# A transformer block on one core: tile 0's modulation and turn done by TensorE, the last turn put inside a down product, one buffer moved

## The reference

```python
mod = (silu(c) @ wmod).reshape(4, 6, 1, 512)          # sa, ca, ga, sb, cb, gb
ga, gb = [(2 * (g >= 0) - 1) * maximum(abs(g), 0.25) for g in (ga, gb)]
h = layernorm(x) * (1 + ca) + sa
q, k, v = heads(h @ w_qkv.T)                           # 16 heads of 32; q, k through relu
vk = sum over tokens of [v; 1] outer k                 # linear attention
out = (vk @ q)[:-1] / ((vk @ q)[-1:] + 1e-15)
x = x + ga * (out @ w_proj.T + b_proj)
h = layernorm(x) * (1 + cb) + sb
w = top-2 of 8 experts by sigmoid(h @ gate_w.T) + router_bias, weights from the sigmoids
x = x + gb * (sum of w_e * silu(h @ W1_e) * (h @ W3_e) @ W2_e + shared expert(h))
```

## Time and profile before

| | |
|---|---|
| median of 3 runs | 1218.91 us (1217.52 to 1221.94) |
| the profiled execution, its own time | 1217.89 us |
| its span from first to last instruction | 1216.1 us |
| mean granted TensorE clock | 0.996 |
| busy: PE, PEld, DVE, ACT, POOL | 98%, 64%, 66%, 34%, 42% |
| first key product / first key and value sums | 25.41 us / 34.97 us |
| experts' stage | about 780 us to the end |

### The profile page before, as it was taken

The page is one execution under the profiler, slowest core; times in us unless marked ns, Lnnn a source line. Parts: engine busy times, 40 slices in busy tenths (PEclk is TensorE's granted clock), DMA queues, the critical chain, the costliest instruction groups (busy, mean ns, idle before and its releaser), DMA issues.

```text
span 1216.1 us, 25326 instructions
## 1 busy us (share of the span) xinstructions
PE 1189.8 (98%) x9054; PEld 776.8 (64%) x9054; DVE 805.9 (66%) x1578; ACT 417.7 (34%) x873; POOL 506.3 (42%) x409
## 2 busy tenths in 40 slices
PE   7999999999999999999999999999999999999996
PEld 2646666666666666767777777656666666666663
DVE  5647778878776777655857754266666666666665
ACT  4424444445443432333323323222222222222221
POOL 2212566656564554222112112345445554455543
PEclk9999999999999999999999999999999999999998
DMA  7816597998788978745434535579787897779783
GB/s 238 228 40 168 125 250 192 214 234 212 182 222 185 229 209 197 173 99 120 122 87 104 137 85 117 111 150 135 132 141 140 131 132 139 138 135 136 133 127 45
DMA packets 253255, 185.27 MB, mean 152 GB/s; under 512 B 186496, under 2 KB 198784, under 8 KB 253132
## 3 DMA queue, kind: packets, MB, share of 16 engines
q1 hardware_dynamic: 217368, 114.40, 42.1%
q0 software_dynamic: 20512, 45.62, 22.4%
q10 hardware_dynamic: 15256, 23.62, 6.7%
HBM read 87.07 MB, written 52.75 MB: 115 GB/s over the span
## 4 chain that ended last, share of the span: by engine, by line
PE 90%; DVE 2%; issue 2%; DMA 2%; POOL 1%; ACT 1%; SPq 0%; ACTq 0%; POOLq 0%; DVEq 0%
PE ps_o L87 7%; PE ps_o L89 7%; PE ps_o L88 7%; PE ps_vs L87 6%; PE ps_vs L88 6%; PE ps_vs L89 6%; PE ps_kh L87 4%; PE ps_vh L87 4%; PE ps_vh L88 4%; PE ps_vh L89 4%; PE ps_kh L88 4%; PE ps_kh L89 4%; PE ps_qh L87 4%; PE ps_qh L89 4%; PE ps_qh L88 4%
## 5 line engine op out<-in xcount | busy, mean ns | idle before, releaser
L444 POOL DMA_INDIRECT out<-y,slot_row x71 | 139.3, 1963 | 190.3 <-DVE y L882 138.7
L89 PE MATMUL ps_o<-w_all,xt 128*128 x568 | 177.5, 313 | 0.0
L88 PE MATMUL ps_o<-w_all,xt 128*128 x568 | 177.5, 313 | 0.0
L87 PE MATMUL ps_o<-w_all,xt 128*128 x568 | 177.5, 312 | 0.0
L874 DVE SCALAR_TENSOR_TENSOR gate_row<-gate_rows,batch_weight,gate_row 128x512 f32<-128x512 f32 x213 | 158.9, 746 | 2.5
L368 POOL DMA_INDIRECT out<-s_sum,row_no x32 | 53.8, 1680 | 197.6 <-DVE s_sum L623 192.0
L1133 ACT ACTIVATE at<-ps_y 128x384 f16<-128x384 f32 x71 | 34.8, 491 | 250.7 <-PE ps_y L1353 247.1
L330 POOL TENSOR_TENSOR h<-cen,rows_f 128x512 f32<-128x512 f32 x32 | 40.6, 1270 | 130.6 <-ACT cen L901 115.4
L89 PE MATMUL ps_qh<-ht,wqkv 128*128 128x128 f16 x512 | 87.4, 219 | 0.0
L88 PE MATMUL ps_qh<-ht,wqkv 128*128 128x128 f16 x512 | 87.4, 219 | 0.0
L87 PE MATMUL ps_qh<-ht,wqkv 128*128 128x128 f16 x512 | 87.4, 219 | 0.0
(11 more groups left out here) (251 smaller groups left out, 3341.2 us busy)
## 6 DMA issues: line engine op xcount, KB each, us to landing
w_stage<-in_w_d ACTq DMA_DIRECT2D x64, 176.0 KB
xb<-in_x SPq DMA_DIRECT2D x32, 256.0 KB, 3.7
xr<-in_x SPq DMA_DIRECT2D x32, 256.0 KB, 4.0
out<-x SPq DMA_DIRECT2D x32, 256.0 KB, 3.6
h_d<-hl SPq DMA_DIRECT2D x32, 256.0 KB, 2.5
h2t_d<-h2t SPq DMA_DIRECT2D x32, 256.0 KB, 3.5
s_ht<-h2t_d SPq DMA_DIRECT2D x32, 256.0 KB, 3.6
sstage<-in_sh_flat SPq DMA_DIRECT2D x32, 136.0 KB, 3.6
```

Source lines behind the costliest of these rows:

```text
L87: nc.tensor.matmul(out, lh, rh, start=first, stop=False, skip_group_check=True)
L88: nc.tensor.matmul(out, lh, rl, start=False, stop=False, skip_group_check=True)
L89: return nc.tensor.matmul(out, ll, rh, start=False, stop=last, skip_group_check=True)
L444: pool.indirect_dma_start(m.out, bass.IndirectOffsetOnAxis(ap=m.slot_row[:, t:t + 1], axis=0), m.y[:, t % Y_RING, :], None, compute_op=ALU ...
```

## The change

Four parts.

1. Modulation. `sct_rep` now holds each of the four batches 32 times (`COPIES`), so that the first set of products gives `sa` and `ca` of all batches. They are copied to a new tile `modrows`; every 32nd partition of it goes to memory. `modulate(0)` and `modulate(1)` are gone. Batch 0's rows are spread over the partitions by two products of one partition of ones with `modrows[0:1]`, into PSUM (`ps_row`).
2. Tile 0. VectorE centres and scales it early ((x - mean) * deviation), then multiplies by and adds the rows from PSUM; GpSimd and ScalarE have no part in it. TensorE turns it in four transposes (`ps_first`), and ScalarE and VectorE split it in two halves straight into `ht` (`turned_high`, `turned_low`). Tile 0 has no DMA transpose. `project_k`, `project_v` and `project_q` of tile 0 wait piece by piece.
3. Order of the start. The loads of all twelve pieces are issued by SP, in a ring of 8 in place of 6, the last four behind waits for `split_low`. The slots -3 to -1 of VectorE and ScalarE are written out by hand, with other places for the splits, `k_low(0)`, `k_high(0)`, `stats(2)`. GpSimd makes `ident` ahead of everything.
4. Experts. `at` is now two tiles: 0 in memory of its own, 1 where both were. `e_high(0)` comes ahead of `first_gate_row(0)`; the wait for the shared expert moves to tile 1. The last turn (tile 70) is made inside the down product of tile 69, behind its first three products, with VectorE's `e_low(70)` ahead of `e_out(69)`.

```diff
     load_x(1)
+    for n in range(KC, 2 * KC):
+        sp.dma_start(m.stage[:, n, :], m.pieces[n][0]).then_inc(m.stage_loaded[n], 16)
     load_x(2)
+    for n in range(2 * KC, 3 * KC):
+        sp.wait_ge(m.stage_lo, n - STAGE_RING + 1)
+        sp.dma_start(m.stage[:, n % STAGE_RING, :], m.pieces[n][0]).then_inc(m.stage_loaded[n % STAGE_RING], 16)
 
...
 
+    def turned_low(half):
+        part = slice(2 * half, 2 * half + 2)
+        v.wait_ge((m.h_half_hi, m.h_hi)[half], 1)
+        v.tensor_tensor(m.ht[:, 0, KC + 2 * half:KC + 2 * half + 2, :], m.ps_first[half],
+                        m.ht[:, 0, part, :], ALU.subtract).then_inc((m.h_half_lo, m.h_lo)[half], 1)
...
-    for s in range(-3, TILES + TAIL):
+    v.wait_ge(m.silu_done, 1)
+    for k in range(KC):
+        v.tensor_copy(m.sct_rep[:, k, :].rearrange("p (b n) -> p b n", b=B), m.sct[:, k, :].unsqueeze(2).to_broadcast([P, B, COPIES])).then_inc(m.rep_done, 1)
+    stats(0)
+    v.wait_ge(m.rstd_done, 1)
+    v.tensor_scalar(m.cen[:, 0, :], m.xb[:, 0, :], m.mv[:, 0, 0:1], m.rstd[:, 0, :], ALU.subtract, ALU.mult).then_inc(m.cen_done, 1)
+    for n in range(KC):
+        split_low(n)
+    stats(1)
+    v.wait_ge(m.bc_done, 2)
+    v.tensor_scalar(m.modrows[:, C:2 * C], m.ps_o[:, 1, :], 1.0, None, ALU.add).then_inc(m.row_done, 1)
+    split_low(4)
+    v.wait_ge(m.spread_done, 1)
+    v.tensor_tensor(m.h[:, 0, :], m.cen[:, 0, :], m.ps_row[CA], ALU.mult).then_inc(m.scaled, 1)
+    v.wait_ge(m.spread_done, 2)
+    v.wait_ge(m.scaled, 1)
+    v.tensor_tensor(m.h[:, 0, :], m.h[:, 0, :], m.ps_row[SA], ALU.add).then_inc(m.h_done, 1)
+    v.tensor_copy(m.rows_f[:, 0, CA, :], m.ps_row[CA]).then_inc(m.rep_done, 1)
+    v.wait_ge(m.rep_done, KC + 1)
+    turned_low(0)
+    turned_low(1)
+    centre(1)
+    for n in range(5, 9):
+        split_low(n)
+    h_low(1)
+    for n in range(9, 12):
+        split_low(n)
+    k_low(0)
+    stats(2)
+    for s in range(TILES + TAIL):
         t = s - LAG
-        if s == -3:
-            v.wait_ge(m.silu_done, 1)
-            for k in range(KC):
-                v.tensor_copy(m.sct_rep[:, k, :], m.sct[:, k, 0:1].to_broadcast([P, P])).then_inc(m.rep_done, 1)
-        if s == -2:
-            v.wait_ge(m.bc_done, 2)
-            v.tensor_scalar(m.rows_f[:, 0, CA, :], m.ps_o[:, 1, :], 1.0, None, ALU.add).then_inc(m.row0_done, 1)
-            v.wait_ge(m.row0_done, 2)
         q_low(s - 1)
         centre(s + 2)
         centre2(t - 2)
         if 0 < s <= TILES and s % BT == 0:
             key_value_sums(s // BT - 1)
         stats(s + 3)
-        if s == -3:
-            for n in range(KC):
-                split_low(n)
-        for n in SPLITS_FIRST.get(s, ()):
-            split_low(n)
         if s == 1:
...
     add(CHUNKS - 1)
     for t in range(1, SLOT_TILES + 1):
-        e_low(t - 1)
+        if t < SLOT_TILES:
+            e_low(t - 1)
         gate_rows_of(t - 1, 1)
         gate_rows_of(t - 1, 2)
         if t < SLOT_TILES:
             e_multiply(t)
         gate_rows_of(t - 1, 3)
+        if t == SLOT_TILES - 1:
+            e_low(t)
...
+    def turned_high(half):
+        part = slice(2 * half, 2 * half + 2)
+        act.wait_ge(m.first_turned, half + 1)
+        act.activation(m.ht[:, 0, part, :], m.ps_first[half], ACT.Copy).then_inc((m.h_half_hi, m.h_hi)[half], 1)
+
...
     act.wait_ge(m.c_loaded, 16)
     act.activation(m.sct[:, :, :], m.ct[:, :, :], ACT.Silu).then_inc(m.silu_done, 1)
-    act.wait_ge(m.wmod_loaded[KC - 1], 16)
-    for n in range(KC, STAGE_RING):
-        load_stage(n)
     for n in range(KC):
         split_high(n)
-    for s in range(-3, TILES + TAIL):
+    act.wait_ge(m.bc_done, 1)
+    act.activation(m.modrows[:, 0:C], m.ps_o[:, 0, :], ACT.Copy).then_inc(m.row_done, 1)
+    split_high(4)
+    split_high(5)
+    turned_high(0)
+    turned_high(1)
+    act.activation(m.rows_f[:, 0, SA, :], m.ps_row[SA], ACT.Copy).then_inc(m.row0_done, 1)
+    scale(1)
+    for n in range(6, 9):
+        split_high(n)
+    h_high(1)
+    split_high(9)
+    split_high(10)
+    k_high(0)
+    split_high(11)
+    for s in range(TILES + TAIL):
         t = s - LAG
-        if s == -2:
-            act.wait_ge(m.bc_done, 1)
-            act.activation(m.rows_f[:, 0, SA, :], m.ps_o[:, 0, :], ACT.Copy).then_inc(m.row0_done, 1)
         logits_out(t - 4)
         q_high(s - 1)
         scale(s + 2)
         scale2(t - 2)
-        if s == -2:
-            load_stage(STAGE_RING)
-            load_stage(STAGE_RING + 1)
-        for n in SPLITS_FIRST.get(s, ()):
-            split_high(n)
         if s == 1:
             act.wait_ge(m.c_loaded, 48)
             act.activation(m.gate[:, :, 0:E], m.gstage[:, :, :], ACT.Copy, scale=SCALE).then_inc(m.stage_hi, 1)
-        k_high(s)
+        if s > 0:
+            k_high(s)
         if s < TILES:
...
     def e_high(t):
         act.wait_ge(m.at_done, t + 1)
-        if t == 0:
+        if t == 1:
             act.wait_ge(m.s_t1_done, 2 * CHUNKS)
         at_least(act, m.ey_done, t - 1)
-        act.activation(m.at[:, t % 2, 0, :, :], m.ps_a[:, :, :], ACT.Copy).then_inc(m.e_at_hi, 1)
+        act.activation(m.at[t % 2][:, 0, :, :], m.ps_a[:, :, :], ACT.Copy).then_inc(m.e_at_hi, 1)
 
     def first_gate_row(t):
         at_least(act, m.ey_ready, t - GW_RING + 1)
@@ -1139,9 +1168,10 @@
         act.activation(m.gate_row[t % GW_RING][:, :], m.gate_rows[:, 0, :], ACT.Copy, scale=m.batch_weight[:, 0, t:t + 1]).then_inc(m.gate_first, 1)
 
     e_silu(0)
-    first_gate_row(0)
     for t in range(1, SLOT_TILES):
         e_high(t - 1)
+        if t == 1:
+            first_gate_row(0)
         first_gate_row(t)
         e_silu(t)
     e_high(SLOT_TILES - 1)
@@ -1150,11 +1180,13 @@
 def tensor_program(nc, m, pe):
     def project_k(i):
         if tile(i):
-            pe.wait_ge(m.ht_loaded[i % HT_RING], ring_use(i, HT_RING))
+            if i >= PE_TURNED:
+                pe.wait_ge(m.ht_loaded[i % HT_RING], ht_use(i))
             at_least(pe, m.k_lo, i)
-            if i == 0:
-                pe.wait_ge(m.stage_lo, KC)
             for k in range(KC):
+                if i == 0:
+                    pe.wait_ge(m.stage_lo, k + 1)
+                    pe.wait_ge(m.h_half_lo if k < 2 else m.h_lo, 1)
...
-            if i == 0:
-                pe.wait_ge(m.stage_lo, 2 * KC)
             for k in range(KC):
+                if i == 0:
+                    pe.wait_ge(m.stage_lo, KC + k + 1)
                 mm = split_matmul(nc, m.ps_v[:, :], (m.ht[:, i % HT_RING, k, :], m.ht[:, i % HT_RING, KC + k, :]),
...
-    modulate(0)
-    pe.wait_ge(m.row0_done, 2)
-    modulate(1)
+    pe.wait_ge(m.consts, ONE_READY)
+    pe.wait_ge(m.row_done, 2)
+    for r in (CA, SA):
+        nc.tensor.matmul(m.ps_row[r], m.one[0:1, :], m.modrows[0:1, r * C:(r + 1) * C], start=True, stop=True).then_inc(m.spread_done, 1)
+    pe.wait_ge(m.h_done, 1)
+    for k in range(KC):
+        mm = nc.tensor.transpose(m.ps_first[k // 2][:, k % 2, :], m.h[:, 0, k * P:(k + 1) * P], m.ident[:, :])
+        if k % 2:
+            mm.then_inc(m.first_turned, 1)
...
         mm.then_inc(m.at_done, 1)
 
-    def e_down(t, expert):
+    def e_down(t, expert, turn_within=False):
         pe.wait_ge(m.e_at_lo, t + 1)
         at_least(pe, m.ey_ready, t)
         for k in range(IT):
...
-            mm = split_matmul(nc, m.ps_ey[:, 0:C], (m.at[0:w, t % 2, 0, k, :], m.at[0:w, t % 2, 1, k, :]),
+            mm = split_matmul(nc, m.ps_ey[:, 0:C], (m.at[t % 2][0:w, 0, k, :], m.at[t % 2][0:w, 1, k, :]),
                               (m.w2[0:w, bass.ds(expert, 1), k, 0, :].rearrange("p o n -> p (o n)"),
                                m.w2[0:w, bass.ds(expert, 1), k, 1, :].rearrange("p o n -> p (o n)")), k == 0, k == IT - 1)
         mm.then_inc(m.ey_done, 1)
 
     pe.wait_ge(m.listed, 1)
     pe.wait_ge(m.w_lo, E * WP)
-    pe.wait_ge(m.consts, CONSTS)
     expert = expert_of(0)
     e_up(0, expert)
     down(CHUNKS - 1)
@@ -1376,9 +1415,8 @@
         e_up(t, following)
         if t == 1:
             pe.wait_ge(m.s_t1_done, 2 * CHUNKS)
-        e_down(t - 1, expert)
+        e_down(t - 1, expert, t == SLOT_TILES - 1)
         expert = following
-    e_turn(SLOT_TILES - 1)
     e_down(SLOT_TILES - 1, expert)
 
...
     sb = region(W_END, END)
     m.a = sb("a", [P, 2, IT * P], F32)
-    m.at = region(GATE_AT, ACT_AT)("at", [P, 2, 2, IT, P], F16)
+    m.at = [(sb, region(GATE_AT, ACT_AT))[j](f"at{j}", [P, 2, IT, P], F16) for j in range(2)]
...
```

More of the change, by code:

```diff
@@ L50 @@
 W_COLS = W13_COLS + IT * 2 * C
-CONSTS = 5
-SPLITS_FIRST = {-2: (4,), -1: (6,), 0: (10, 11)}
-SPLITS_LAST = {-2: (5,), -1: (7, 8, 9)}
+IDENT_READY, ONE_READY, V_READY, HEADS_READY = 3, 4, 6, 11
+PE_TURNED = 1
+COPIES = P // B
 PAIR_RING = 4
@@ L89, in split_matmul, with ht_use @@
     return nc.tensor.matmul(out, ll, rh, start=False, stop=last, skip_group_check=True)
+def ht_use(i):
```

(25 more changed lines are left out.)

77 lines of the change are left out of this document (39 added, 38 removed).

## The result

The changed kernel takes 1221.62 us (median of 22 runs, 1218.62 to 1227.14), the kernel before 1218.06 in 22 runs beside it (1215.14 to 1221.94). The ratio is 1.003, 95% interval 1.0022 to 1.0039: slower, by less than the 0.5% that I count as a difference, but beyond the interval. The profiled execution has a span of 1219.1 us against 1216.1, which is +3.0 where I had +0.5.

The account below looks back on a forecast made before the run. TensorE, busy 98% of 1216 us, bounds the kernel, so only start, first expert tile or end can gain. Terms -0.1 + 1.65 - 0.97 - 0.1 = +0.5 on the median 1218.91 gave 1219.4 us, range 1214.5 to 1223.

Parts of the forecast that it names:

- signs of being wrong: Prediction counts as wrong if the first `ps_vs` product starts before 33.5, or if a later stage waits anew.
- the 4.3 us: Start: first key product at 21.1, 4.3 us sooner, lost again because tile 0's sums wait for VectorE's low part of v 0.
- the order of the start: Tile 0's key and value sums start at 34.9 against 34.97 before: gain 0.1 us, between -0.1 and 1.5.
- the clock: TensorE's granted clock falls in or behind the 4.2 us idle stretch ahead of tile 0's sums: +1.65 us, bounds 0 and 3.0.
- the loads: Start: the twelve pieces on the sync queue land before 20, wanted from 24 on: nothing.
- rival c: Slower: tile 1's low part of v late by more than 1.3 us, a second clock fall 1.65 more: about 1223; chance 0.08.
- the first expert tile: Tile 0's down product starts 1.76 us sooner, but the gate row is late next: -0.97 us, bounds 0.84 and 1.76.
- the end: Last turn inside the down product saves 1.26 us of waiting, but three gate rows remain: gain 0.1, between 0 and 0.3.

Follow-up runs that it names:

- run 9: The changed kernel with low and high part of v 0 ahead of tile 2's statistics, loads left in place: 1222.16 us, ratio 1.0038 to the kernel before.
- run 3: The changed kernel with 18 unused products on TensorE ahead of the first sums, to hold the clock: 1221.35 us, ratio 1.0034 to the kernel before.
- run 6: The changed kernel with 4 MB of modulation weights loaded early by SP, plus 18 unused products holding the clock: 1219.03 us, ratio 1.0007 to the kernel before.
- run 10: The changed kernel with ScalarE's modulation weight loads one slot later (slots 1 and 2): 1218.95 us, ratio 1.0011 to the kernel before.
- run 2: The changed kernel with SP's wait for the stored modulation rows moved to their read-back in slot 2: 1226.5 us, ratio 1.0074 to the kernel before.
- run 5: The changed kernel with 4 MB of modulation weights loaded by SP right behind the twelve pieces: 1219.99 us, ratio 1.0012 to the kernel before.
- run 1: The kernel before with the expert edits alone (`at` in two tiles, `e_high(0)` earlier, last turn inside the down product): 1216.66 us, ratio 0.9991.

## Why the prediction was off by what it was

The sum had +0.5, the medians say +3.56. The time lies inside the range, but above the 1218 to 1221 that I called likeliest, and it is the width of the range that holds it, not the sum. One of my own signs of being wrong has come, a later stage that waits anew: 0.94 us ahead of k 3.

**Right: little comes of it, since the 4.3 us are lost again.** The first key product came at 21.52 (I had 21.1; the four turns ahead of it took 1.11 us here, 0.66 in run 9), TensorE stood 4.03 us (about 4.2) ahead of the sums, and these waited for VectorE's low part of v 0. Run 9 shows that this wait was real and its cause right: with that part ahead of the statistics the sums start at 29.05.

**Right in mechanism, off in size: the order of the start, -0.1 in my sum, +0.63 measured.** Sums at 35.60, not 34.9; the upper bound was 35.1. The chain of tile 2 is what was mis-sized. Centre 2 ended at 30.94 (I had 30.7), but GpSimd's deviation, which began beside it at 30.34, took 1.01 us and ended at 31.35, 0.41 behind the centre; alone it takes 0.55 in the same trace (33.46) and would have ended with the centre. I had the row of the split beside a shift and didn't apply it here. That the Trainium skill's rule (SBUF — State Buffer, section "SBUF: two separate sides") was the better price can be read off: it added 0.4, measured are 0.41. The deviation took 1.01 or 1.02 us in all ten traces with the changed start. The rest is 0.24 ahead of the end of centre 2, and some 0.15 in the hand-overs from there to the low part of h 2, which began at 34.20 where I had 33.4. A caution belongs to the +0.63: the sums of tile 0 start at 34.97 and 34.33 in the two traces with the old start, and at 34.53 to 35.70 in the seven with the new start and this order, so a difference of this size between two single executions is hardly more than their scatter.

**Right: the clock, +1.65.** From sums 0 to k 2 the changed kernel takes 1.65 longer, with 0.59 granted over 36 to 40. Runs 3 and 6, which fill the idle stretch, keep 1.00 there. That the size came out to the hundredth is partly luck: of the four traces with this idle stretch, two show 1.65 and 1.66 (after and run 10) and two 2.89 and 2.83 (runs 2 and 5), near my upper bound.

**Wrong: the loads, 0 in my sum, +1.70 measured.** The prediction wrote of the queues "nothing" each time: it looked at whether the pieces land in time and whether tile 1's transpose does, and saw ScalarE's loads only as 0.9 us of issuing that delays a centre (rival c). It didn't ask what else is in flight when tile 2's transpose goes out. The order of two issues turned, from 0.63 ahead of 2 MB to 0.35 behind their start; the transpose of tile 2 then landed after 10.3 us in place of 4.5, the store behind it after 11.3 in place of 6.4, and the transpose of tile 3 went out 6.3 us later. Runs 5 and 10 take the 1.70 away by moving the loads in either direction; run 9 shows that TensorE gains next to nothing by being sooner while they lie there. By run 1 the order alone isn't enough: there the transpose landed after 10.0 us and cost nothing. In the changed kernel the whole chain is late as well, with the transpose issued 2.1 us later than in run 1 and the store 1.9, and the slack of some 0.7 us doesn't cover that. Of the 1.70, 0.94 are a wait for the turned rows of tile 3 and 0.42 one for the low part of v 2, behind a wait of ScalarE for `sstage` (4.41 us); the other 0.34 lie in the last product ahead of each wait, which shows as 0.22 us where the next one otherwise starts after 0.06. My rival (c) had the sign and nearly the time (1223 against 1221.6), but by another mechanism (low part of v 1 late by more than 1.3 us), and that didn't happen: the sums of tile 1 start 9.21 behind k 1, 1.35 more than before, without any wait in between: that is the slower clock.

**Right: the first expert tile, -0.97 in my sum, -0.83 measured** (-0.94 in run 1). The down product starts without a wait, `e_high(0)` is no longer behind the gate rows, and the gate rows' landing is next, which delays the multiplication of tile 1. The timeline of the changed kernel shows it:

```profile
799.43 1.33 ACT L1168 ACTIVATE gate_row<-gate_rows,batch_weight 128x512 f32<-128x512 f32 x2 [2.99 <-DMA gate_rows<-mod_d]
...
801.64 0.52 DVE L893 SCALAR_TENSOR_TENSOR a<-ps_o,a 128x352 f32<-128x352 f32 x1
...
802.22 0.55 PE L1391 MATMUL ps_y<-ident,a 128*128 128x128 f32 x3 [0.77 <-DVE a L893]
```

**Right: the end, -0.1, measured -0.09.** The wait for the turn went, and one of 0.98 us for `y` of tile 69 stands ahead of the last down product in its place, in run 1 as well; `y` of tile 69 at 1206.87 and the last gate rows behind it (1207.48) set the end.

By the sum +2.91 of +3.0 in the profiled execution is accounted for. The medians of the runs lie 3.56 apart.

## What to carry to other kernels

When a change moves a small, urgent DMA (a transpose above all) by even a microsecond, list what every other queue issues within a few microseconds of it: going out just behind a bulk load made it land 6 us later here, which was free where that much slack was left and cost 1.7 us where it wasn't. A sooner start of the first product is worth nothing until each link behind it is sooner too; look for the wait that ends last (here a low part behind another tile's chain on VectorE, and then a transpose behind loads), and undo both together: here neither alone beat the kernel before. A wait that a chain names can be a symptom: moving it made this kernel slower.
